# A three-block decoder layer on one core: who stores the empty rows, in what order the first unit's parts are written and read, and when the second unit is projected

## The reference, cut to what matters

```python
x = x + self_attention(layernorm(x), Wq, bq, Wk, bk, Wv, bv, Wo, bo)   # 16 heads of 16, 3D rope on q and k
x = x + cross_attention(ctx, ctx, layernorm(x), mask, W_fc)            # ctx is keys and values
x = x + experts(layernorm(x))                                          # 8 experts of 256 -> 1024 -> 256, top 2
```

## Time and profile before

| | us |
|---|---|
| Median of 3 runs | 708.97 |
| Lowest and highest | 708.71, 710.58 |
| The profiled execution | 709.13 |
| Its span | 707.3 |
| PE busy in the span | 664.6 |
| POOL busy in the span | 273.6 |

### The profile page before, as it was taken

How to read it: one execution, slowest core, us unless ns; L and a number is a source line. 1 busy time by engine, 2 the same in 40 slices (tenths; PEclk the granted TensorE clock), 3 DMA queues, 4 the chain that set the end, 5 groups by cost and what they waited for, 6 DMA issues and landing times.

```text
span 707.3 us, 16309 instructions
## 1 busy us (share of the span) xinstructions
PE 664.6 (94%) x5099; PEld 519.4 (73%) x5099; DVE 481.5 (68%) x1319; ACT 431.8 (61%) x849; POOL 273.6 (39%) x597
## 2 busy tenths in 40 slices
PE   8887999999999999999989999986999999999996
PEld 4555576666766657666556688976999999999995
DVE  2496787685876887868872526245878787878781
ACT  3444657567575688778566587752656565656551
POOL 4233325354234455544274353563322222222322
PEclk9999999999999999999999999997999999999998
DMA  5545445544465454765587532222222222222212
GB/s 136 145 116 158 116 136 152 156 147 136 143 158 162 145 162 135 224 190 152 143 336 275 183 124 54 63 73 54 39 41 39 40 39 40 39 40 39 40 24 23
DMA packets 52381, 81.72 MB, mean 116 GB/s; under 512 B 9213, under 2 KB 41801, under 8 KB 51273
## 3 DMA queue, kind: packets, MB, share of 16 engines
q1 hardware_dynamic: 42441, 67.76, 33.0%
q0 software_dynamic: 7536, 10.69, 8.4%
q10 hardware_dynamic: 2320, 2.23, 0.9%
HBM read 54.80 MB, written 25.51 MB: 114 GB/s over the span
## 4 chain that ended last, share of the span: by engine, by line
PE 70%; POOL 9%; DVE 7%; issue 6%; ACT 4%; DMA 3%; SPq 1%; DVEq 0%; ACTq 0%; POOLq 0%
PE attention_psum L770 17%; PE attention_psum L777 15%; PE attention_psum L762 7%; PE attention_psum L712 6%; PE attention_psum L731 6%; PE attention_psum L810 4%; PE attention_psum L667 4%; PE attention_psum L656 4%; PE attention_psum L661 4%; POOL ordered_rows L1468 3%; DMA out<-over 2%; PE attention_psum L848 2%; DVE neg_max L1257 2%; ACT weights L953 1%; PE attention_psum L820 1%
## 5 line engine op out<-in xcount | busy, mean ns | idle before, releaser
L1257 DVE TENSOR_REDUCE neg_max<-attention_psum 128x2 f32<-128x512 f32 x256 | 165.3, 682 | 35.7 <-PE attention_psum L712 35.3
L939 ACT ACTIVATE weights<-attention_psum 128x512 f32<-128x512 f32 x256 | 147.3, 595 | 64.1 <-PE attention_psum L731 53.3
L770 PE MATMUL attention_psum<-over,v 128*128 128x128 f32 x1248 | 149.0, 278 | 8.9 <-DVE over L1309 8.8
L1026 ACT ACTIVATE weights<-attention_psum,b_sb 128x128 f32<-128x128 f32 x312 | 89.0, 369 | 111.8 <-PE attention_psum L770 111.8
L770 PEld LDWEIGHTS attention_psum<-over,v 128*128 128x128 f32 x1248 | 147.4, 194 | 12.0 <-DVE over L1309 9.9
L777 PE MATMUL attention_psum<-weights 128*128 x624 | 141.3, 379 | 0.1
L1547 POOL DMA_INDIRECT out<-over x39 | 63.1, 1618 | 182.5 <-DVE over L1326 175.0
L1309 DVE STREAM_TRANSPOSE over<-over 32x64 f32<-32x64 f32 x496 | 116.8, 236 | 15.5 <-DMA over<-ordered_rows 9.2
L777 PEld LDWEIGHTS attention_psum<-weights 128*128 128x128 f32 x624 | 115.7, 190 | 14.7 <-issue 0.4
L712 PE MATMUL attention_psum<-weights 99*128 99x256 bf16 x512 | 98.7, 275 | 7.1 <-DVE neg_max L1257 6.8
L731 PE MATMUL attention_psum<-weights 102*128 102x256 bf16 (+1 forms) x512 | 101.9, 273 | 2.2 <-ACT weights L939 1.2
(11 more groups left out here) (180 smaller groups left out, 769.0 us busy)
## 6 DMA issues: line engine op xcount, KB each, us to landing
parts<-weights SPq DMA_DIRECT2D x96, 128.0 KB
weights<-parts SPq DMA_DIRECT2D x64, 192.0 KB
weights<-parts SPq DMA_DIRECT2D x64, 128.0 KB
weights<-in_L_ffn_w SPq DMA_DIRECT2D x8, 1024.0 KB, 6.8
over<-ordered_rows SPq DMA_DIRECT2D x39, 136.0 KB, 2.1
weights<-parts SPq DMA_DIRECT2D x64, 64.0 KB
w_sb<-in_L_ffn_w SPq DMA_DIRECT2D x8, 512.0 KB, 3.8
weights<-in_L_ffn_w SPq DMA_DIRECT2D x8, 512.0 KB, 5.2
```

The source lines that it names most:

```text
L770: last = pe.matmul(m.hT_bank[j % 2][:, c * P:(c + 1) * P], m.w1t[j % 2][:, k, c * P:(c + 1) * P], m.xT[j % 2][:, k, :], start=(k == 0), st ...
L939: act.activation(m.p[:, u % P_RING, :], m.b_bank[u % B_RING], ACT.Exp, scale=SCALE[ORDER[u // H][0]]).then_inc(m.b_free[u % B_RING], 1)
L1026: last = act.activation(m.hidT[n % HIDDEN][:, c, :], m.hT_bank[n % 2][:, c * P:(c + 1) * P], ACT.Gelu, bias=m.b1_sb[:, bass.ds(gelu_expert ...
L1257: v.tensor_reduce(m.neg_max[:, :, h:h + 1], m.a_bank[u % A_RING].rearrange("p (t k) -> p t k", t=T), AXX, ALU.max, negate=True).then_inc(m ...
```

## The change

The empty rows are stored by SyncE with eight plain transfers at rows that it reads from the table `m.pad`; POOL keeps the memset and the row numbers, in an earlier slot. Tile loads 7 to 10 are put into the slots by the same rule as the later ones. Unit 0's six parts are stored in turn, q and k, by a piece of their own, and its k stacks are loaded by ACT's queue. k's third part of unit 0 is computed by DVE. Most pieces of unit 1 up to `v` come before slot 0. The first loads are reordered, sequence 2 is loaded among them, and three entries of `WARM` are smaller.

```diff
--- before.py
+++ after.py
@@ -110,15 +110,14 @@
         "read", 1, 1), (11, "max", 0), (11, "max_parts", 0), (11, "max_rows", 0), (15, "max_parts", 1), (17,
         "max", 1), (20, "max_rows", 1))
 
-FIRST_AT = ((-31, "ln_a", 0), (-30, "ln_d", 0), (-29, "turn"), (-28, "qk_a", 0), (-27, "qk", 0), (-25, "qk_a", 1), (-24,
-        "qk", 1), (-23, "rope", 1), (-22, "v", 0), (-20, "rope", 0), (-19, "roped", 0), (-19, "roped", 1), (-18,
-        "v", 1), (-18, "stack", 0), (-17, "rest", 0), (-16, "stack", 1), (-15, "mid", 0), (-15, "rest", 1),
-        (-15, "write", 0), (-15, "mid", 1), (-15, "write", 1), (-12, "read", 0, 0), (-12, "read", 1, 0), (-4,
-        "read", 1, 1), (-3, "read", 0, 1))
-SECOND_AT = ((-12, "ln_a", 0), (-11, "ln_d", 0), (-8, "turn"), (-4, "qk_a", 0), (-3, "qk", 0), (-3, "qk_a", 1), (-3, "rope",
-        0), (-2, "qk", 1), (-2, "rope", 1), (-1, "roped", 0), (0, "v", 0), (1, "stack", 0), (1, "v", 1), (1,
-        "roped", 1), (1, "rest", 0), (3, "mid", 0), (3, "write", 0), (3, "stack", 1), (4, "rest", 1), (4, "mid",
-        1), (4, "write", 1), (5, "read", 0, 0), (9, "read", 1, 0), (13, "read", 1, 1), (14, "read", 0, 1))
+FIRST_AT = ((-31, "ln_a", 0), (-30, "ln_d", 0), (-29, "turn"), (-28, "qk_a", 0), (-27, "qk", 0), (-26, "rope", 0), (-25, "qk_a",
+        1), (-24, "qk", 1), (-23, "rope", 1), (-22, "roped", 0), (-22, "roped", 1), (-21, "v", 0), (-20, "v", 1),
+        (-18, "stack", 0), (-17, "rest", 0), (-16, "stack", 1), (-15, "mid", 0), (-15, "rest", 1), (-15, "mid", 1),
+        (-14, "first_write"), (-12, "read", 0, 0), (-12, "read", 1, 0), (-4, "read", 1, 1), (-3, "read", 0, 1))
+SECOND_AT = ((-21, "ln_a", 0), (-15, "ln_d", 0), (-14, "turn"), (-13, "qk_a", 0), (-13, "qk", 0), (-12, "rope", 0), (-12, "qk_a",
+        1), (-11, "qk", 1), (-10, "rope", 1), (-9, "roped", 0), (-9, "roped", 1), (-8, "v", 0), (-8, "v", 1),
+        (1, "stack", 0), (2, "rest", 0), (3, "stack", 1), (4, "mid", 0), (4, "rest", 1), (5, "write", 0),
+        (5, "mid", 1), (6, "write", 1), (8, "read", 0, 0), (9, "read", 1, 0), (14, "read", 1, 1), (15, "read", 0, 1))
 
 FIXED_AT = (-24, -3, 8)
 
@@ -141,7 +140,7 @@
         "o_move", 0), (37, "o_move", 1), (39, "ot", 0), (40, "ot", 1), (41, "cturn"), (44, "proj_a"), (45,
         "proj"), (45, "ln_a", 2), (48, "store"), (55, "ln_d", 2), (57, "rturn"), (58, "logits")))
 
-WARM = ((10, "top", 0, 0), (26, "turn", 0, 0), (2, "max", 0, 0, 0), (9, "stack", 0, 0, 0), (4, "max", 0, 0, 1), (30,
+WARM = ((10, "top", 0, 0), (15, "turn", 0, 0), (2, "max", 0, 0, 0), (2, "stack", 0, 0, 0), (4, "max", 0, 0, 1), (2,
         "turn", 0, 1), (2, "turn", 0, 2), (2, "qk", 0, 2, 1), (2, "max", 0, 3, 1), (8, "turn", 0, 4), (3, "max",
         0, 4, 1), (7, "turn", 0, 5), (6, "max", 0, 5, 1), (4, "turn", 0, 6), (3, "max", 0, 6, 1), (10, "cturn",
         0, 7), (8, "turn", 0, 7), (2, "ot", 0, 7, 0), (12, "max", 1, 0, 1), (1, "rturn", 1, 1), (6, "max", 1, 1,
@@ -178,7 +177,7 @@
         (296, "up_a", 2), (297, "up_b", 2), (297, "rows", 6), (298, "down_a", 1), (299, "up_a", 3), (299, "meta", 4),
         (300, "down_b", 1), (300, "moved_y", 1), (302, "xturn", 4), (302, "down_a", 2), (302, "w1t", 4),
         (302, "add", 1), (302, "down_b", 2), (302, "up_b", 3), (302, "meta", 5), (303, "moved_y", 2),
-        (303, "add", 2), (303, "rows", 7), (305, "rows", 8))
+        (303, "add", 2))
 
 STEADY, STEADY_AT = 3, 304
 
@@ -270,11 +269,10 @@
         for name, ahead in (("rows", 4), ("meta", 3), ("w1t", 2), ("xturn", 2), ("up_a", 1), ("up_b", 1),
                             ("down_a", 0), ("down_b", 0), ("moved_y", 0), ("add", 0)):
 
-            if j + ahead < N_TILES and (name != "rows" or j + ahead > EARLY + 1):
+            if j + ahead < N_TILES:
                 slots[STEADY_AT + j - STEADY].pieces.append((name, TILE, j + ahead))
-            if name == "rows" and j in (EARLY - 3, EARLY - 2):
-                slots[STEADY_AT + j - STEADY].pieces.append((name, TILE, j + 3))
-    slots[POS[CROSS, B - 1] * H + LAG + 46].pieces.append(("padded", CROSS, B - 1))
+    slots[POS[CROSS, B - 1] * H + LAG + 27].pieces.append(("empty", CROSS, B - 1))
+    slots[STEADY_AT + 1].pieces.append(("padded", CROSS, B - 1))
     return [slots[at] for at in range(first, last)]
 
 
@@ -456,7 +454,7 @@
 
         self.s_out = [sem(f"stored_out{i}") for i in range(2)]
         self.s_dve, self.s_pool = sem("dve_chain"), sem("pool_chain")
-        self.s_route_const, self.s_empty, self.s_bias = sem("route_consts"), sem("empty_rows"), sem("b1_turned")
+        self.s_route_const, self.s_blank, self.s_empty = sem("route_consts"), sem("blank_made"), sem("empty_rows")
         self.s_exp_in, self.s_exp = sem("route_exp_in"), sem("route_exp")
         self.s_chosen, self.s_place, self.s_before = sem("chosen"), sem("places"), sem("counts_before")
         self.s_listed = [sem(f"listed{b}") for b in range(len(BATCH_ENDS))]
@@ -513,14 +511,16 @@
     x_t = x.rearrange("b (t p) d -> p (b t) d", p=P)
     c_t = ctx_in.rearrange("b (t p) d -> p (b t) d", p=P)
     sp.dma_start(m.rows_of(0), x_t[:, 0:T, :]).then_inc(m.s_x[0], 16)
-    for i, w in enumerate((wq, wk, wv)):
+    for i, (w, b) in enumerate(((wq, bq), (wk, bk), (wv, bv))):
         sp.dma_start(m.wqkv[:, :, i * D:(i + 1) * D],
                      w.rearrange("(c p) n -> p c n", p=P)).then_inc((m.s_wq, m.s_wk, m.s_wv)[i], 16)
-    for i, b in enumerate((bq, bk, bv)):
+        if i == 0:
+            sp.dma_start(m.table[:, :, :, :],
+                         rope.rearrange("(t p) (a d) -> p t a d", p=P, a=2)).then_inc(m.s_qkv, 16)
         sp.dma_start(m.bias_qkv[:, i * D:(i + 1) * D],
                      b.rearrange("(a d) -> a d", a=1).broadcast_to([P, D])).then_inc(m.s_qkv, 16)
-    sp.dma_start(m.table[:, :, :, :], rope.rearrange("(t p) (a d) -> p t a d", p=P, a=2)).then_inc(m.s_qkv, 16)
     sp.dma_start(m.rows_of(1), x_t[:, T:2 * T, :]).then_inc(m.s_x[1], 16)
+    sp.dma_start(m.rows_of(2), x_t[:, 2 * T:3 * T, :]).then_inc(m.s_x[2], 16)
     sp.dma_start(m.bias_o[:, :], bo.rearrange("(a d) -> a d", a=1).broadcast_to([P, D])).then_inc(m.s_small, 16)
     sp.dma_start(m.r_bias[:, 0:E], router_b.rearrange("(a d) -> a d", a=1).broadcast_to([P, E])).then_inc(m.s_small, 16)
     sp.dma_start(m.r_bias[:, E:E + L],
@@ -538,7 +538,7 @@
             if name == "setup":
                 sp.wait_ge(m.s_setup_v, 3)
                 sp.dma_start(neg.rearrange("r (g p) -> g r p", p=P), m.neg[0:NT + T]).then_inc(m.s_neg, 16)
-            elif name == "x":
+            elif name == "x" and n > 2:
                 sp.dma_start(m.rows_of(n), x_t[:, n * T:(n + 1) * T, :]).then_inc(m.s_x[n], 16)
             elif name == "bias":
                 sp.dma_start(m.b1_sb[:, :, :], b1.rearrange("e (p c) -> p e c", c=FC)).then_inc(m.s_b, 16)
@@ -557,7 +557,13 @@
                     sp.wait_ge(made, i + 1)
                     sp.dma_start(parts[i, w, part].rearrange("d h s -> h d s"),
                                  m.parts[w][:, part, :]).then_inc(m.s_write[w], 16)
-            elif name == "read":
+            elif name == "first_write":
+                for part, cast in enumerate((m.s_hi, m.s_mid, m.s_third)):
+                    for w in range(2):
+                        sp.wait_ge(cast[w], 1)
+                        sp.dma_start(parts[0, w, part].rearrange("d h s -> h d s"),
+                                     m.parts[w][:, part, :]).then_inc(m.s_write[w], 16)
+            elif name == "read" and (i > 0 or piece[3] == 0):
                 w, half = piece[3:]
                 r = i % STACKS
                 if i >= STACKS:
@@ -612,6 +618,12 @@
                     sp.wait_ge(m.b_full[u % B_RING], u // B_RING + 1)
                     sp.wait_ge(m.s_values, len(ORDER) * H - P_RING // 2)
                 sp.dma_start(m.w2_sb[:, n, :, :], w2[n].rearrange("(p c) d -> p c d", c=FC)).then_inc(m.s_w2, 16)
+            elif name == "padded":
+                sp.wait_ge(m.s_blank, 1)
+                sp.wait_ge(m.s_routed, 2)
+                for e in range(E):
+                    row = sp.value_load(m.pad[0:1, e:e + 1], min_val=0, max_val=E * REGION - P)
+                    sp.dma_start(ordered[bass.ds(row, P), :], m.empty).then_inc(m.s_empty, 16)
             elif name == "rows":
 
                 if n == 0:
@@ -921,7 +933,7 @@
                 last.then_inc(m.fills(piece), 1)
 
 
-def scalar_attention(m, out):
+def scalar_attention(m, out, parts):
 
     act, plan = m.nc.scalar, m.plan
     out_t = out[0:NT * P, :].rearrange("(t p) d -> p t d", p=P)
@@ -972,6 +984,15 @@
             elif name == "setup":
                 act.wait_ge(m.s_const, 2)
                 act.dma_start(out[NT * P:NT * P + P, :], m.zeros).then_inc(m.s_zero, 16)
+            elif name == "read" and i == 0 and piece[3] == 1:
+                half = piece[4]
+                act.wait_ge(m.s_fixed, 1)
+                act.wait_ge(m.s_write[1], 16 * PARTS)
+                for block, many, part, step in K_LOADS:
```

(26 more changed lines are left out.)

## The result

The changed kernel took 699.1 us in the median of 4 runs, where the kernel before took 709.6 us in the runs beside it. The ratio is 0.9855, with a 95% interval of 0.9825 to 0.9884: 10.4 us less. The forecast was 692.9, within 689 to 698. The direction was right, the size was 6 us off, and the time lies above the range.

What follows compares the result with a forecast made beforehand. PE was taken to bound the kernel (busy 94% of the span), so only its stands pay. From 709.13 us, 11.3 for the tile stage and 4.9 for the first stage gave 692.9, range 689 to 698.

Steps and rivals of the forecast that it cites:

- the tile stage: Moving POOL's eight empty-row stores to SyncE removes PE's 8.77 us stand before tile 9 and 2.51 at half clock: 11.3 us.
- C: Tile stage: SyncE's stores are slow, at 4 us each 6 us of standing are left, 701 us; chance 0.03.
- D: Tile stage: each store holds SyncE's queue 7.2 us until landed, stall 22.5 us longer, 726.7 us; chance 0.02.
- the list of signs: Signs to check in the new profile, among them tile 9's load issued near 447 us.
- Steps 1 to 3: First turn about 8.8, gain 1.8; first stack 19.08 to about 15.8; unit 0's q reads at 24.3, k reads at 25.2.
- Step 4: ACT's queue with six k reads, and PE at half clock, both put unit 2's turn at 35.2: gain 4.9 us.
- What I weighed at 17 to 21 us: First stage: with fewer fillers PE stands 4 us, its clock falls, and first scores start near 33.1 instead of 30.8.
- Rival A: The first stage gives nothing: ACT's blocked issues and half clock keep unit 2's turn at 40; 697.8 us, chance 0.13.
- rival B: PE's half clock after 61 us goes away, worth 1.6, or the first stage gives 7: 690.8, both 689.2; chance 0.10.

Runs made afterwards that it cites:

- e4: The changed kernel with 18 fillers instead of 2 ahead of unit 1's turn and 8 instead of 2 ahead of unit 2's: 696.6 us, ratio 0.9808.
- e5: e4 with the nine loads of b1 and b2 on SyncE's queue 96 slots earlier: 701.5 us, ratio 0.9807 to the kernel before.
- e3: The changed kernel with 18 fillers instead of 2 ahead of unit 1's turn: 696.9 us, ratio 0.9824 to the kernel before.
- g1: The changed kernel itself, unaltered, run again as a base for its variants: 709.8 us, ratio 0.9869 to the kernel before.

## Why the prediction missed

- **What bounds the kernel, and the tile stage: right.** POOL's eight stores were the stall, 8.77 us of standing and 2.5 at half clock. Forecast 11.3, measured 11.4 between the profiles and 11.9 by the stores-only kernel. That SyncE had 16 us to spare was right (15 measured), and so rivals C and D fell. Two readings were off without touching the sum: 464.37 and 474.28 are the starts of the first and the last of POOL's stores, seven steps, so 1.42 us each on average and not 1.27; and tile 9's load went out at 455.1, where the working had 452.3 + 0.83 and the list of signs 447.
- **Steps 1 to 3 of the first stage: right.** First turn 8.8 (8.88), first stack 15.8 (16.1), q's reads 24.3 (24.8), k's 25.2 (25.5).
- **Step 4: the path was the wrong one.** "PE waits for the last" of ACT's queue: it was DVE's moments of unit 2, held by the projections at half clock, and the turn came 2.1 us later than my 35.2. I had let the half clock reach the first scores (33.1, measured 32.9) and not followed it into DVE's order. The 2.1 us that I allowed from there to the turn had no row: the kernel before took 5.1, and PE's own work alone took 3.0.
- **The failed step.** "From slot 4 on the same DVE work is left, so 61.10 moves by the same 4.9." DVE's work was the same, but PE's was not at the same clock. I took DVE's 17.09 of 17.70 us as cover for PE, whose 13.77 us in the same row would have shown that the cover is gone once PE takes double. What I weighed at 17 to 21 us happened again at 37: the granted clock was 0.50 until 47.5, and PE's projections took 1.7 us for four where they take 0.9 at the full clock. The stretch from turn to turn took 25.0 us in place of 21.0. Of these 4.0 us the fall cost 3.4 (25.0 against 21.6 in e4 and e5, where no fall came before 51), and the other 0.6 is not explained. The Trainium skill, "TensorE: Matmul & The Clock Gate", section "HAM oscillation — how this bites in real kernels", says that an array that waits for long loses the full clock and that the work behind pays. The trace agrees on the price, but here the fall came with a stand of only 1.3 us in a sparse stretch, shorter than the waits of which that section tells, and the measurement decides.
- **A second one behind it.** "Everything from there to 475 is mostly PE's own work, and moves with its start." From 305 to 335 it follows SyncE's queue. Had the forecast's 4.9 been there at slot 20, most of it would have been lost there, as far as the runs tell: e4 brought 4.5 to the stretch and had 0.9 behind it, e3 4.1 and 1.8.
- Rival A came near the time (697.8, measured 699.1) and had part of the cause: half clock, but not ACT's queue, as the k reads on SyncE show. Its unit 2's turn at 40 did not come either: that was 37.3, and the gain was lost behind it. Its time was also the top of the range, with no room for a loss behind it. The first half of rival B came true beside it: in all four profiles with the changed front the clock does not fall after 60.

What stays open: what decides when and for how long the clock falls, as it differs between executions of the same code; why one SyncE issue in many takes 1.2 to 1.7 us in that stretch, where the median is 0.59, and whether the first stage without fillers is worth zero or costs a microsecond (1.0015, 0.9995 to 1.0035).

The new front with both rows of fillers and the early loads has the lowest ratios: 0.9807 and 0.9799 of the kernel before, against 0.9855 and 0.9869 for the changed kernel. With the late loads the same front had 0.9808 in the first group and 0.9834 in the third, so only the third sets the two apart.

## What to carry to other kernels

A gain at the front has to be followed to the end: look for every later stretch in which another engine or queue has no gap, because it takes back what comes early. When an engine seems to cover another by being busier, check the cover again at the other's slower clock before fillers are taken away. A stall in the last stage, behind every such stretch, is worth its full length.

## What the runs showed of the hardware

A fall of the clock does not need a long stand: in the changed kernel it came in a stretch of sparse work with a stand of 1.3 us. The falls seen in the first 70 us lasted from 3 to 10 us, and their places and lengths differ between executions of the same kernel: 20 to 27 and 37 to 47.5 us in the changed kernel's profile, 23 to 26 and 37 to 46 in g1. SyncE's issues of the same kind of stack read range widely (changed kernel; ns, min/median/max):

```profile
L584 SPq DMA_DIRECT2D weights<-parts x186: 537/587/1629, 24.8 to 351.1; - x186
```

Eight stores of 128 rows at a row read from a register cost SyncE 1.05 us each with the register work, where POOL's indirect form took 1.42 from start to start on average, and mostly 1.3. In all profiles of the second, third and fourth groups DVE and ACT also stand, for up to 5 us at a time between about 359 and 380 us, and DVE once more for 5 to 7 us between about 445 and 460, for what the trace calls remote; a row of DVE's timeline of e5 is below. The kernel before, the changed kernel and the first group's kernels have no such wait. Two of ACT's copies around the first of these stands, at 360 and 370 us in the kernel before, are 10.2 us apart there and 16.5 to 17.1 in the later groups, so it is much of what made these slower, and nothing that I tried explains it.

```profile
363.11 0.69 DVE L1278 TENSOR_REDUCE neg_max<-attention_psum 128x2 f32<-128x512 f32 x1 [3.82 <-remote]
```
